# Two graph layers with experts on one core: edge incidence spread from transposed local destinations, X's sum shared out in routing, ranks by repeated maxima, rows placed four at a time

## The reference

```python
# 1: attention over the edges, 4 heads of 64
h = (ln(x) @ W).reshape(N, 4, 64)
e = leaky_relu(a_src[src] + a_dst[dst], 0.2)
e = exp(e - segment_max(e, dst)[dst])
x = x + segment_sum(e / segment_sum(e, dst)[dst] * h[src], dst) + bias
# 2: 6 experts of three layers, the best 2 of each row
rh = relu(ln(x) @ router_w1 + b1)
top_w, top_i = top_k(softmax(rh @ router_w2 + b2), 2)      # ties: the lower index
x = x + sum_k softmax(top_w)[k] * expert[top_i[k]](ln(x))
# 3: attention over the same edges, 1 head of 256, with 64 edge attributes in the score
# 4: 8 experts of three layers, all of them for each row, weighted by a softmax
```

## Time and profile before

| | us |
|---|---|
| median of 3 runs | 4315.09 (4308.82 to 4315.14) |
| profiled execution, its time | 4308.81 |
| profiled execution, its span | 4307.1 |

### The profile page before, as it was taken

The page is one execution under the profiler, slowest core; times in us unless marked ns, Lnnn a source line. Parts: engine busy times, 40 slices in busy tenths (PEclk is TensorE's granted clock), DMA queues, the critical chain, the costliest instruction groups (busy, mean ns, idle before and its releaser), DMA issues. The chain is left out here.

```text
span 4307.1 us, 73738 instructions
## 1 busy us (share of the span) xinstructions
PE 3250.0 (75%) x15898; PEld 2470.8 (57%) x15898; DVE 2923.0 (68%) x9596; ACT 1554.4 (36%) x4357; POOL 2021.3 (47%) x2122
## 2 busy tenths in 40 slices
PE   6466666676766789964566666666668999999999
PEld 4244444444444578853344444444447888888888
DVE  5599999999997867655566666666657765454554
ACT  3233333333332224432333333333323333434343
POOL 3777777777770034446777777777740000000000
PEclk9577777777776579987677777777779999999999
DMA  5444444444464146744444444444452000000000
GB/s 147 102 109 108 108 106 106 106 107 107 106 98 89 39 108 191 190 128 123 108 108 108 108 109 108 108 108 108 108 64 76 6 8 5 7 5 7 5 7 8
DMA packets 379249, 372.18 MB, mean 86 GB/s; under 512 B 246016, under 2 KB 305580, under 8 KB 378634
## 3 DMA queue, kind: packets, MB, share of 16 engines
q0 software_dynamic: 99072, 273.04, 25.7%
q1 hardware_dynamic: 277994, 94.55, 10.0%
q10 hardware_dynamic: 1818, 0.74, 0.1%
HBM read 326.48 MB, written 41.60 MB: 85 GB/s over the span
## 5 line engine op out<-in xcount | busy, mean ns | idle before, releaser
L782 POOL DMA_INDIRECT g_G<-rows,g_pack x1856 | 1754.9, 946 | 627.7 <-issue 497.2
L815 PE MATMUL bank<-g_G,g_MB 128*125 128x260 f32 x1856 | 670.6, 509 | 248.0 <-DVE acc L1023 246.7
L1023 DVE SCALAR_TENSOR_TENSOR acc<-acc,g_c,bank 125x65 f32 (+1 forms) x2320 | 617.4, 315 | 134.9 <-DVE acc L1023 67.2
L815 PEld LDWEIGHTS bank<-g_G,g_MB 128*125 128x125 f32 x1856 | 426.7, 248 | 392.0 <-DVE acc L1023 284.2
L815 PE MATMUL bank<-g_G,g_M 128*125 128x257 f32 x1856 | 631.2, 487 | 20.5 <-DVE acc L1023 20.3
L1321 ACT ACTIVATE e_h<-bank,bn_shift,bn_scale 128x250 f32<-128x250 f32 x800 | 400.6, 555 | 531.5 <-PE bank L1274 411.1
L886 ACT ACTIVATE g_mt_d<-bank,unode 125x256 bf16<-125x256 f32 x928 | 380.9, 460 | 437.1 <-PE bank L800 436.9
L815 PEld LDWEIGHTS bank<-g_G,g_M 128*125 128x125 f32 x1856 | 417.1, 241 | 145.8 <-DVE acc L1023 25.6
L1445 DVE SCALAR_TENSOR_TENSOR X<-bank,e_cw,X 125x256 f32 (+1 forms) x400 | 175.1, 479 | 408.4 <-PE bank L1283 406.4
L1283 PE MATMUL bank<-e_w,e_h 128*125 128x256 f32 x1400 | 334.0, 382 | 20.5 <-ACT e_h L1321 16.3
L898 ACT ACTIVATE g_MT<-g_mt_d,ones 125x512 bf16<-125x512 bf16 x464 | 335.0, 722 | 11.4
(11 more groups left out here) (326 smaller groups left out, 4539.6 us busy)
## 6 DMA issues: line engine op xcount, KB each, us to landing
g_G<-rows,g_pack POOLq DMA_INDIRECT x1856
acc<-in_edge_attr SPq DMA_DIRECT2D x50, 476.0 KB
g_pack<-edge_pack SPq DMA_DIRECT2D x928, 2.0 KB
g_drow<-edge_dst SPq DMA_DIRECT2D x928, 1.0 KB
expert_out<-x_y SPq DMA_DIRECT2D x54, 256.0 KB
g_qe<-edge_q SPq DMA_DIRECT2D x464, 1.0 KB
rows<-acc SPq DMA_DIRECT2D x25, 227.5 KB
rows<-n_T SPq DMA_DIRECT2D x25, 224.9 KB
```

Of the source, the lines that this page charges most:

```text
L782: nc.gpsimd.indirect_dma_start(G[:, r, q, :], None, rows_d[l], bass.IndirectOffsetOnAxis(ap=pack[:, r, q, 0:1], axis=0)).then_inc(S(p + f" ...
L815: mm_ = nc.tensor.matmul(sum_bank(r, k, u)[0:TN, 0:HW], left, G[:, rk, q, :], start=(c == 0), stop=(c == C - 1))
L1023: ins = nc.vector.scalar_tensor_tensor(at, at, c1[:, rk, u, h:h + 1], sum_bank(r, k, u)[0:TN, h * W:(h + 1) * W], ALU.mult, ALU.add)
```

## The change

1. Spread. `edge_dst`, `hl` and `drow` are gone, with their stores and their eight loads a slot. ScalarE copies `LT` once more, to bf16 (`LTb`), and TensorE spreads single rows of it by a one-hot column `pick_row`: four matmuls of 128 columns in place of one of 512. The bias is the node number within the tile, the same for all units, so one activation of 512 elements does for two of 256. The scan on VectorE overwrites `LT` and so waits for `LTb`.
2. Layer 0's rows: SyncE issues the slot with the last load of `X` before the store of the edge table, not after it.
3. Routing: one of the two tiles of a group is scaled by ScalarE (four activations), the sum into `X` is made by GpSimd, and the stages lag further behind each other (up to five slots, before three). SyncE waits for the small router tables before it asks for the experts' weights. Each first product is made twice: first into bank 7, which nothing reads, then into its own bank.
4. Sorting: the ranks come from two rounds of maximum and equality on 125x300 elements. The placing loop handles four row choices at once in two buffers, in bf16, with the row number split into partition and tile: VectorE marks, ScalarE weighs, TensorE places. The tile table of the experts is made behind the marks.
5. Dense experts: the statistics of the second group (`finish(1)`, `root`) come before `normal_shares(0, 0)`, and the first group's exponentials (`weigh(0)`) before the first activations of expert 1.

```diff
-                                sp.dma_start(drow[:, u, :], dst_d[:, bass.ds(s, UE)]).then_inc(S(p + f"drow_in{(r - 1) % RING}"), 16)
...
                             if v_ == 0:
-                                pe.wait_ge(S(p + f"drow_in{r1}"), filled(t, r, 1, 16 * U))
+                                pe.wait_ge(S(p + "LTb"), i)
...
-                            nc.tensor.matmul(bank[2 + v_ % 2][0:TN, :], ones_bf[:, :], drow[:, 2 * v_:2 * v_ + 2, :].rearrange("k u e -> k (u e)"),
-                                             start=True, stop=True).then_inc(S(p + "spread"), 1)
+                            for k in range(CP):
+                                row = (v_ * CP + k) * H
+                                mm_ = nc.tensor.matmul(bank[2 + v_ % 2][0:TN, k * P:(k + 1) * P], pick_row[:, row:row + 1].broadcast_to([QH, TN]), LTb[:, :],
+                                                       start=True, stop=True)
+                            mm_.then_inc(S(p + "spread"), 1)
...
+                            nc.scalar.activation(mt_d[:, v_ % 2, :, :], bank[2 + v_ % 2][0:TN, :].rearrange("p (q e) -> p q e", q=CP), ACT.Abs,
+                                                 bias=minus_n[0:TN, :]).then_inc(S(p + "mt_abs"), 1)
...
                             nc.scalar.copy(LT[:, :], rowT_ps[:, P:2 * P]).then_inc(S(p + "LT"), 1)
+                            if late(i, 2):
+                                act.wait_ge(S(p + "spread"), i * V - V)
+                            act.wait_ge(S(p + "LT"), i)
+                            nc.scalar.copy(LTb[:, :], LT[:, :]).then_inc(S(p + "LTb"), 1)
...
                             v.wait_ge(S(p + "FB"), i)
+                            v.wait_ge(S(p + "LTb"), i)
...
+                        slot(NG - 5, (NG - 5) % 4, (NG - 5) // 4)
                         sp.wait_ge(S("pack_made"), 1)
...
+                    sp.wait_ge(S(p + "w"), 16 * 6)
                     for w, name in zip((w1, w2, w3), ("L0_ffn_expert_w1", "L0_ffn_expert_w2", "L0_ffn_expert_w3")):
...
+                            nc.gpsimd.tensor_tensor(xt, xt, y[:, r, :, :], ALU.add).then_inc(S(p + "x"), 1)
...
+                            for k in range(2):
+                                nc.tensor.matmul(bank[7][:, 0:GN], wr[:, k, :], xnT[:, r1, k, :], start=(k == 0), stop=(k == 1))
+                            for k in range(2):
+                                mm = nc.tensor.matmul(bank[2 + r1][:, 0:GN], wr[:, k, :], xnT[:, r1, k, :], start=(k == 0), stop=(k == 1))
+                            mm.then_inc(S(p + "rh_mm"), 1)
...
+                            for h in range(H):
+                                k = i * GT + GT - 1
+                                ins = nc.scalar.activation(y[:, r, GT - 1, h * DH:(h + 1) * DH], acc[:, bass.ds(k * HW + h * W, DH)], ACT.Copy, scale=den[:, bass.ds(k * H + h, 1)])
+                            ins.then_inc(S(p + "y_act"), 1)
...
+                    def first_best(from_, out):
+                        step(nc.vector.tensor_tensor(code[:, :, :], from_, wide(top[:, :]), ALU.is_equal))
+                        step(nc.vector.tensor_tensor(code[:, :, :], code[:, :, :], early[:, :].unsqueeze(1).broadcast_to([TN, NT, NX]), ALU.mult))
+                        step(nc.vector.tensor_reduce(top[:, :], code[:, :, :], AX.X, ALU.max))
+                        step(nc.vector.tensor_tensor(out, code[:, :, :], wide(top[:, :]), ALU.is_equal))
+
+                    first_best(ex[:, :, :], pick[:, 0, :, :])
+                    step(nc.vector.scalar_tensor_tensor(rest[:, :, :], pick[:, 0, :, :], -2.0, ex[:, :, :], ALU.mult, ALU.add))
+                    step(nc.vector.tensor_reduce(top[:, :], rest[:, :, :], AX.X, ALU.max))
+                    first_best(rest[:, :, :], pick[:, 1, :, :])
...
+                        if late(h, 2):
+                            v.wait_ge(S(p + "hot"), h - 1)
+                            v.wait_ge(S(p + "placed"), h - 1)
...
+                        nc.scalar.activation(hot_hi[:, r, :, 0, :], is_hi[:, r, :, :], ACT.Copy, scale=nid[0:TN, 0:1])
+                        for k in range(2):
+                            ins = nc.scalar.activation(hot_hi[:, r, 2 * k:2 * k + 2, 1, :], is_hi[:, r, 2 * k:2 * k + 2, :], ACT.Copy, scale=tid[:, bass.ds(h * 2 + k, 1)])
+                        ins.then_inc(S(p + "hot"), 1)
```

More of the change, by code:

```diff
@@ L729, in _ @@
                 def _(sp):
-                    regs = [[sp.alloc_register(f"{p}start{k}_{u}") for u in range(U)] for k in range(2)]
+                    regs = [sp.alloc_register(f"{p}start{u}") for u in range(U)]
                     def slot(i, r, t):
-                        if not has(i, 0) and not has(i, 1):
+                        if not has(i, 0):
                             return
@@ L755, in slot @@
[L755 to L763 removed]
+                        sp.reg_load(regs, unit_i[0:1, bass.ds(i * U, U)])
@@ L1572, in _ @@
+                        if grouped(i, 4):
+                            pe.wait_ge(S(p + "rhT"), i - 3)
+                            if late(i, 6):
+                                pe.wait_ge(S(p + "lg"), i - 5)
+                            for u in range(GT):
+                                mm = nc.tensor.matmul(bank[4 + r2][0:TN, u * 16:u * 16 + NX], rhT[:, r2, u * TN:(u + 1) * TN], wr2[:, :], start=True, stop=True)
+                            mm.then_inc(S(p + "lg_mm"), 1)
                     run(pe, slot)
```

271 lines of the change are left out of this document (125 added, 146 removed).

## The result

The changed kernel takes 4258.88 us (median of 4 runs, 4257.96 to 4259.76), the kernel before 4313.27 in the same session: a ratio of 0.9873, 95% interval 0.9861 to 0.9885, so 54 us faster. The profiled executions differ by less, 4307.1 against 4258.0 us of span, 49.1 us.

What follows compares the result with a forecast made beforehand. GpSimd's gather issuing was taken to pace the second attention (floor 20.1 us a slot), a TensorE-VectorE ring the first. Terms of -38.3 us gave 4270.5 from the profiled 4308.8, 4276.8 from the median; forecast 4273, range 4253 to 4296.

Steps and rivals of the forecast that it cites:

- part 1: First rows stage: three VectorE operations gone, -2.1 us, and no idle for the last X load, -3.0; sum -5.
- part 2: Both attentions: gathers keep setting the second's pace, added TensorE work stays hidden except in the last slots; +0.5 us.
- part 3: Routing: earlier start and 3.1 us a group at full clock instead of 3.64, less lag and clock rise; -11 us.
- part 4: Sorting: ranks -5 us, placing at 1.6 us a pass instead of 2.25, -14.5; sum -19.5.
- part 5: Last stage: statistics moved into the first gap and exponentials asked for earlier shorten waits of VectorE and TensorE; -3.3 us.
- TensorE the bound: Routing's steady part: at full clock TensorE's products, transposes and logits set the period of 3.1 us a group.
- Rival C: GpSimd's addition and VectorE hinder each other in routing, for the addition's whole length: +8 us, 4281; chance 0.10.
- B: Rival: the clock stays at half in routing, 5.5 us a group, 4328 us in all; chance 0.07.
- F: Rival: VectorE's wait at L1110 goes from 0.70 to 1.61 us in every slot: +53 us, 4326; chance 0.03.
- E: Rival: the first attention's slots shorten to the gathers' floor: -17 us, 4256; chance 0.04.
- the ring of two: Placing in sorting: with two buffers a pass waits for the one two before; 3.2 us for two passes.
- D: Rival: placing does not speed up, as each pass crosses three engines: 2.25 us a pass, 4288; chance 0.04.

Runs made afterwards that it cites:

- b_orders: The kernel before with two SyncE orders changed: edge table's stores behind one more X load, experts' weights asked for after the router's small tables; 4302.04 us.
- a_single: The changed kernel without the unread product of the routing stage; 4263.61 us.
- b_double: The kernel before with the router's first product made twice, once into an unread bank, and nothing else; 4309.22 us.
- a_y_later: The changed kernel with VectorE making routing's normalized rows before the product y, and adding the router's bias after the aggregates; 4257.63 us.
- best: The changed kernel with routing reordered on VectorE and ScalarE, and VectorE's wait in placing split between ScalarE's and TensorE's use of the buffer; 4286.13 us.

## Why the prediction was right, step by step

The sign, the two large terms and the range were right. By stage, parts 1 and 2 with the means above, the others from the two profiled executions:

| term | forecast | measured |
|---|---|---|
| part 1, first rows stage | -5 | -7.5 |
| part 2, both attentions | +0.5 | -5.0 |
| part 3, routing | -11 | -16.5 |
| part 4, sorting | -19.5 | -18.5 |
| part 5, last stage | -3.3 | -3.4 |
| sum | -38.3 | -50.9 |

4259 lies 14 us below the forecast of 4273, inside the range. 12.6 us of that are the terms: parts 1 to 3 gained 2.5, 5.5 and 5.5 us more than forecast, part 4 gained 1 us less.

**Part 1.** The term was undersized. By the one trace of b_orders the store's move gave 3.7 us against 3.0, and the table's removal 3.8 against 2.1. -7.5 lies 0.3 beyond my bound of -7.2. The idle time for `X` is gone from the changed kernel's list of waits, as forecast.

**Part 2** is the term that failed, by 5.5 us and in sign. "In the second attention the gathers go on setting the pace" held for all of them but one. The step that failed is the 20.1 us a slot, "which I take for the floor": the gathers' own pace is 20.0 (16 x 1.250), and what the mean of 1.257 had beside it is one wait of 6.40 us for TensorE, ahead of the last eight gathers. The change brought it to 2.62 us. GpSimd's list of waits hid it, because it counts the 0.30 us that stand before every gather as well: 36.6 us for TensorE in 100 waits before, 31.6 in 96 after, and one of them is the 6.4 and the 2.6. That the new spreads shorten it is shown by fourteen traces; which of their halves does is not. "Only in the last slots, with no gathers behind them, does a longer ring show: +0.5" fits: 0.9 us behind the last gathers.

**Part 3.** The clock was right, and a_single and b_double show that the unread product makes it. "TensorE the bound" was wrong, though the 3.1 us a group came out: without two long periods at the start the mean is 3.09, with them 3.21. TensorE is 84% busy and waits for VectorE's rows. VectorE is busy 2.6 us a group where I had 2.1, 0.3 of it by the lock, and its chain waits another 0.36 for ScalarE. That the wrong engine gave the right number is luck.

The start gave 5.4 against 4. From the first statistics to the last, 24 periods, the stage fell from 88.8 to 77.1 us, so -11.7. My terms for that were -13.5 for the rate, +5 for two groups at half clock and +2 for the lag (with the start of -4 they make -10.5, where I wrote -11). The +7 was the mis-sized term. Only one long period, of 5.06 us, goes with half clock: ScalarE waited 2.06 us for the product during which the clock rose, VectorE 1.93 us for the square root behind it, and then y met the addition (1.37 us). The next, of 3.96, lies wholly at full clock and is a wait that I had not thought of, for the store of the rows four groups earlier:

```profile
1367.82 0.74 DVE L1641 TENSOR_SCALAR r_xn<-X,r_ag,r_rs 125x256 f32<-125x256 f32 x2 [1.33 <-DMA expert_in<-r_xn]
```

The first three periods, still at half clock, are 2.54 to 2.57 us, while the slots fill, and the two long ones are together 2.8 us above 3.09 each. The rate itself was worth more than I had: before's mean period was 3.70 us, not the 3.64 of the one group that I read.

**Rival C** was half true. The lock is there in 16 of 25 groups (L1631 at 0.69 in its median, 0.3 us above 0.42 in the mean), but it costs the rest of the addition, not its whole length, and taking it from y gave back only 2.8 us (a_y_later). The operation at 29.52 that I named for the rule is a cast with one SBUF input, so it is not the pair that I quoted; y is. B fell: from 1370 to 1430 us the clock is 1.00. F fell: from 200 to 1280 us the successor of L1110 waits 38.8 us in 52 slots, before 40.3 in 53. E gave a seventh of its size in the first attention, 2.3 of 17 us.

**Part 4.** Ranks -5.1 against -5. Placing, from the end of the positions to the result, 58.0 before and 44.5 now, -13.5 against -14.5: the ring of two that I had at 3.2 us for two passes measures 3.41. best shows it was that ring: with VectorE's wait split, it is 1.32 a pass. D fell. (My 40 and 3 us make 43, not the 43.5 that I subtracted.)

**Part 5.** As forecast in this pair of executions: 1069.0 to 1065.6 us, and the wait fell from 3.82 to 1.25 us. Seven traces of each order give 4.0 us in the mean.

**The starting point.** I reckoned from 4308.8, the profiled run, and from the median. The six first stages show that the profiled run was 1.7 us quick in that stage alone.

## What to carry to other kernels

A wait that covers two buffers is two waits: where an instruction stands behind the release of both, but needs only one, splitting it opened a ring of three engines and took 0.38 us off each of 25 passes. Before work is moved to another engine, write down the ring through its inputs, slot by slot; one slot more of lag was the difference between 102 and 180 us of routing. The mean distance of a busy engine's instructions is not its floor: look at the distances one by one. Here 926 of 927 were equal and the one that was not, in the last slots of the stage, held the whole gain; no steady slot shows it. In a list of waits, read the longest beside the sum.

## What the hardware showed that I had not expected

- At the end of the second attention the DMA share was 1.01, against 0.45 in the slots ahead of it, and VectorE waited 12.14 us for gathered rows, before the change, and 9.82 after it.
- Added work with an unread result, 1.01 us a group at full clock, made a stage 4 to 7 us shorter by the clock alone; TensorE's busy share was lower with the full clock (83 to 84%) than with the half (96 to 98%).
- GpSimd's addition on 125x512 elements holds not only VectorE's product of two tensors (0.42 to 1.37 us) but also its scaling of one tensor by two columns (0.40 to 1.05 us); a reciprocal of 2 elements inside the same addition kept its 0.17 us.
- A loop of identical code took 2.04 or 2.24 us a pass in kernels that differ only elsewhere in the program: 5 us of 25 passes, as much as a whole part of this change. A difference of this size in a stage that a change does not touch is no evidence for or against it.
